# Attention loop of a convolution-and-attention kernel on one core: where sums, maxima and loads stand in the queues of each engine

## The reference, cut to what matters

```
q_in = quantile(x, 0.5) over the pixels;  x = x + relu(-q_in)
y = down2(relu(up2(x)))                       # 7-tap separable filter
spec = rfft2(y); gate = sigmoid(gelu(|spec| w1) w2); xf = y + irfft2(spec * gate)
q = xf @ q_w + q_b
k, v = two strided convolutions of xf (8x8 and 16x16), layer norm, kv_w, depthwise 3x3 on v
attn = softmax(q k / 4);  out = attn v @ proj_w + proj_b + y
```

## Time and profile before

| what | value |
|---|---|
| median of 3 runs | 11078.33 us (11071.28 to 11083.63) |
| the profiled execution's own time | 11074.85 us |
| span of its trace | 11073.5 us |
| instructions | 198462 |
| mean granted TensorE clock | 0.956 of 2.4 GHz |
| PE, DVE, ACT, POOL busy | 90%, 78%, 65%, 53% of the span |

### The profile page before, as it was taken

How to read it: one execution, slowest core, us unless ns; L and a number is a source line. 1 busy time by engine, 2 the same in 40 slices (tenths; PEclk the granted TensorE clock), 3 DMA queues, 4 the chain that set the end, 5 groups by cost and what they waited for, 6 DMA issues and landing times. The chain is left out here.

```text
span 11073.5 us, 198462 instructions
## 1 busy us (share of the span) xinstructions
PE 9980.4 (90%) x68713; PEld 4898.6 (44%) x68713; DVE 8648.7 (78%) x14529; ACT 7156.8 (65%) x12301; POOL 5870.6 (53%) x10577
## 2 busy tenths in 40 slices
PE   1998998989989899899989989899898998989989
PEld 1534535344353543535335353453534435354353
DVE  7877778877778777778777787777787777877777
ACT  5756666666666756667566675666667566675665
POOL 2374463745637365472754737446374553736547
PEclk9999999999999999999999999999999999999999
DMA  2031231312314032140322303123131331413214
GB/s 64 25 77 50 55 89 29 78 39 64 80 32 89 26 74 71 38 91 35 72 56 49 96 21 79 48 58 87 32 79 36 66 79 32 89 33 71 67 41 104
DMA packets 330611, 664.69 MB, mean 60 GB/s; under 512 B 95624, under 2 KB 241160, under 8 KB 308048
## 3 DMA queue, kind: packets, MB, share of 16 engines
q1 hardware_dynamic: 329552, 651.29, 24.7%
HBM read 232.53 MB, written 71.30 MB: 27 GB/s over the span
## 5 line engine op out<-in xcount | busy, mean ns | idle before, releaser
L1328 ACT ACTIVATE R<-ps 128x512 f32<-128x512 f32 x5120 | 2876.0, 593 | 1480.6 <-PE ps L816 1040.6
L1104 DVE TENSOR_REDUCE R<-ps 128x2 f32<-128x640 f32 x3840 | 3031.9, 818 | 757.6 <-PE ps L795 709.0
L269 ACT ACTIVATE R<-R,st 128x1475 bf16<-128x1475 f32 (+2 forms) x1326 | 2014.6, 1519 | 440.3 <-DVE st L343 415.0
L332 DVE TENSOR_SCALAR_CACHE_REDUCE R<-R,st 128x1255 bf16<-128x1255 f32 (+2 forms) x1326 | 2014.9, 1520 | 19.5 <-DVE st L343 0.2
L795 PE MATMUL ps<-KST,R 96*128 96x320 bf16 x7680 | 1703.0, 303 | 42.5 <-DMA R<-R 25.9
L841 PE MATMUL ps<-R 128*32 128x512 f32 x12288 | 1671.3, 617 | 0.0
L816 PE MATMUL ps<-R,KST 104*128 104x512 bf16 x4096 | 1599.3, 393 | 37.4 <-DMA R<-Wk 28.6
L1425 POOL TENSOR_TENSOR R<-R 128x256 f32<-128x256 f32 x1440 | 1054.6, 732 | 115.3
L1429 POOL TENSOR_TENSOR R<-R 128x256 f32<-128x256 f32 x1440 | 1046.9, 727 | 120.1
L795 PEld LDWEIGHTS ps<-KST,R 96*128 96x128 bf16 x7680 | 711.3, 99 | 759.0 <-DVE R L1104 283.0
L816 PEld LDWEIGHTS ps<-R,KST 104*128 104x128 bf16 x4096 | 396.9, 97 | 1083.6 <-ACT R L1328 748.6
(11 more groups left out here) (226 smaller groups left out, 19694.3 us busy)
## 6 DMA issues: line engine op xcount, KB each, us to landing
R<-R SPq DMA_DIRECT2D x3072, 64.0 KB, 2.4
R<-xh_in SPq DMA_DIRECT2D x136, 512.0 KB, 4.4
out_dram<-Z SPq DMA_DIRECT2D x68, 1024.0 KB, 3.9
R<-Wk SPq DMA_DIRECT2D x960, 64.0 KB, 2.0
Wk<-Wk SPq DMA_DIRECT2D x960, 64.0 KB, 2.0
R<-xa_in SPq DMA_DIRECT2D x36, 1024.0 KB, 10.0
R<-xb_in SPq DMA_DIRECT2D x36, 1024.0 KB, 11.7
R<-sr_in SPq DMA_DIRECT2D x32, 1024.0 KB, 5.0
```

The lines of the kernel that those rows point to most:

```text
L269: e.activation(junka[:, 2047:2048] if k == LONE else junka[:, 0:o2 - o1], xc[:, o1:o2], ACT.Sign, bias=mid, scale=-1.0, accum_out=ca[i]).t ...
L332: e.tensor_scalar(junk[:, 0:o1 - o0], xc[:, o0:o1], mid, None, ALU.is_le, ALU.add, accum_out=cv[i]).then_inc(md_cv, 1)
L1104: e.tensor_reduce(MX[(4 * u + s4) % 2][:, blk_, h0:h0 + 2], ps[:, 2 + 2 * bq:4 + 2 * bq, 0:320], axis=AX.X, op=ALU.max).then_inc(mx, 1)
L1328: e.activation(PB[:, t % 2, w, :], ps[:, w % 2, :], ACT.Exp).then_inc(ex, 1)
```

## The change

What it does, part by part:

1. On PE, `lay_max(t + 1)` moves from slot 0 to slot 3, on ACT from slot 1 to slot 3, and on DVE `split_max` moves from slot 8 of the tile before to slot 2 of the tile.
2. In SP's step, `lay_out(t - 1)` becomes the first thing, then come the loads of images, two DMAs of `load_unit`, then `lay_max(t + 1)`, then the remaining DMAs of `load_unit`.
3. The normalised sums get two buffers NO, the projection is of tile t - 4 and stands in slot 0, and `rest(t - 4)` in slot 2. The buffers ON and OX move to Wk.
4. The last three tiles, not two, are turned and divided by PE and DVE and need no `lay_out` or `normalise`; the first of them is divided at slot 3 of the last tile, ahead of the magnitudes (`largest`).
5. Unit 2 is loaded in steps 2 to 4 and unit 3 in steps 5 to 7, eight DMAs each; the first half of the image is loaded in two parts, at steps 28 and 29. The `stage` calls move by two slots.
6. Ahead of the loop, `slot` stands behind every second product of TAP1 and behind groups of six of TAP2, the first maxima are interleaved otherwise, and some `busy` products on the identity are added.

```
@@ constants
-STAGES = {(0, 2): (1, 0, 6), (0, 6): (1, 1, 6), (1, 2): (1, 2, 6), (1, 6): (1, 3, 6),
-          **{(8 * g - 12 + j, 2): (g, j, 6) for g in (2, 3) for j in range(4)}}
+STAGES = {(0, 4): (1, 0, 6), (0, 8): (1, 1, 6), (1, 4): (1, 2, 6), (1, 8): (1, 3, 6),
+          **{(8 * g - 12 + j, 4): (g, j, 6) for g in (2, 3) for j in range(4)}}
-LOADS = {u: 2 if u == 2 else 4 * u - 8 for u in range(2, 8)}
+LOADS = {**{3 * u - 4 + i: (u, 8 * i, 8 * i + 8) for u in (2, 3) for i in range(3)},
+         **{4 * u - 8 + i: (u, 6 * i, 6 * i + 6) for u in range(4, 8) for i in range(4)}}
+TURNED = 3
@@ tensor, keys
-                if n in (1, 3, 5):
-                    stage(0, n // 2 + 1, (4, 5, 3)[n // 2])
-                slot(1 if n > 5 else 0)
+                slot(n % 2)
+                if n in (3, 9, 15):
+                    stage(0, n // 6 + 1, (4, 5, 3)[n // 6])
@@ tensor, attention loop
-                    if w == (0 if t else 4) and t + AHEAD - 1 < NT:
+                    if w == 0 and t > 3:
+                        project_out(t - 4)
+                    if w == 3 and t + AHEAD - 1 < NT:
                         lay_max(t + AHEAD - 1)
                     if w in WEIGHS and t:
                         weigh(t - 1, WEIGHS.index(w))
-                    if w == 5 and t > 2:
-                        project_out(t - 3)
@@ vector, attention loop
-                    if w == 7 and t > 2:
-                        rest(t - 3, True)
+                    if w == 2 and t and t + AHEAD - 1 < NT:
+                        split_max(t + AHEAD - 1)
+                    if w == 2 and t > 3:
+                        rest(t - 4, True)
                     if w < 8 and ahead < NT:
                         maxima(ahead // 4, ahead % 4, w)
-                    if w == 8 and ahead < NT:
-                        split_max(ahead)
                     if w == 8 and t:
                         sums(t - 1)
@@ scalar, attention loop
-                    if w == (1 if t else 4) and t + AHEAD - 1 < NT:
+                    if w == 3 and t + AHEAD - 1 < NT:
                         lay_max(t + AHEAD - 1)
@@ gpsimd
                 if t:
-                    e.wait_ge(po_ps, t)
+                    e.wait_ge(on, t)
+                if t > 1:
+                    e.wait_ge(po_ps, t - 1)
...
-                e.tensor_tensor(XN2, XO[k], XI, ALU.mult).then_inc(on, 1)
+                e.tensor_tensor(NO[k], XO[k], XI, ALU.mult).then_inc(on, 1)
@@ sync, attention loop
-                if t + AHEAD - 1 < NT:
-                    lay_max(t + AHEAD - 1)
+                if 0 < t <= NT - TURNED:
+                    lay_out(e, t - 1)
+                if t >= NT - 4 and t < NT - 2:
+                    e.wait_ge(sc_ps, 280)
+                    load_next(e, it, 0, part=t - NT + 4)
...
-                if u == 7 and s4 == 0:
-                    e.wait_ge(sc_ps, 280)
-                    load_next(e, it, 0)
-                for v, t0 in LOADS.items():
-                    if t0 <= t < t0 + 4:
-                        load_unit(e, v, 6 * (t - t0), 6 * (t - t0) + 6)
-                if 0 < t < NT - 1:
-                    lay_out(e, t - 1)
+                v, n0, n1 = LOADS.get(t, (0, 0, 0))
+                if n1:
+                    load_unit(e, v, n0, n0 + 2)
+                if t + AHEAD - 1 < NT:
+                    lay_max(t + AHEAD - 1)
+                if n1:
+                    load_unit(e, v, n0 + 2, n1)
```

More of the change, by code:

```diff
@@ L156, in program @@
         XD = [R2[:, 1024 + 256 * i:1280 + 256 * i] for i in range(2)]
-        XI, XN2, ON, OX = (R2[:, 1536 + 256 * i:1792 + 256 * i] for i in range(4))
+        XI, XN2, *NO = (R2[:, 1536 + 256 * i:1792 + 256 * i] for i in range(4))
+        ON, OX = W[:, 1536:1792], W[:, 1792:2048]
         RD = [R2[:, 2640 + 16 * i:2656 + 16 * i] for i in range(2)]
@@ L877, in tensor @@
             lay_max(0)
-            for k in range(16, 20):
+            for k in range(14, 20):
                 first_maxima(k)
+                busy(0, 1)
+            busy(0, 4)
             for t in range(NT):
@@ L1081, in vector @@
                 stage(0, j, (6, 4, 5, 3)[j])
-                slot((4, 4, 4, 13)[j])
+                slot((3, 3, 4, 6)[j])
             first, second = keys(0), keys(1)
             next(first)
-            slot(1)
+            slot(3)
             next(first)
-            slot(1)
+            slot(3)
             next(first, None)
-            slot(1)
-            for k in range(8):
+            slot(6)
+            for k in range(4):
                 first_maxima(k)
             next(second)
-            first_maxima(8)
-            first_maxima(9)
+            first_maxima(4)
+            first_maxima(5)
             next(second)
-            first_maxima(10)
+            first_maxima(6)
+            first_maxima(7)
             next(second, None)
-            for k in range(11, 20):
+            for k in range(8, 20):
                 first_maxima(k)
@@ L1279, in keys @@
                              ACT.Identity, bias=c(f"v{n}b", 64)).then_inc(ka[s], 1)
+                yield
                 if s == 0:
@@ L1296, in scalar @@
             next(first)
-            bias(56, 64).then_inc(zb, 1)
+            bias(25, 37)
+            next(first)
+            bias(37, 52)
+            next(first)
+            bias(52, 62)
             next(first, None)
-            next(second)
-            next(second, None)
+            bias(62, 64).then_inc(zb, 1)
+            for _ in range(4):
+                next(second, None)
             def lay_max(t):
@@ L1307, in lay_max, with turned @@
                 e.activation(MR[t % 2], pb[0:8, :], ACT.Copy).then_inc(mr, 1)
+            def turned(t):
+                n = t - NT + TURNED
+                e.wait_ge(ot_ps, n + 1)
+                if n:
+                    e.wait_ge(po_ps, t)
+                e.activation(OX, ps[:, 4 + t % 2, 0:256], ACT.Copy).then_inc(ox, 1)
             def values():
@@ L1334, in scalar @@
                         stage(*STAGES[t, w])
-            for n in range(2):
-                e.wait_ge(ot_ps, n + 1)
-                if n:
-                    e.wait_ge(po_ps, NT - 2 + n)
-                e.activation(OX, ps[:, 4 + n, 0:256], ACT.Copy).then_inc(ox, 1)
+                    if t == NT - 1 and w == 7:
+                        turned(NT - 3)
+            turned(NT - 2)
+            turned(NT - 1)
         def gpsimd(e):
```

108 lines of the change are left out of this document (66 added, 42 removed).

## The result

The changed kernel takes 15283.25 us (median of 4 runs, 15278.3 to 15285.26) against 11078.11 us (11071.28 to 11083.63, 4 runs) for the kernel before: a ratio of 1.3797 [1.3779, 1.3814]. That is 4205 us more, 262.8 for each of the 16 images. The forecast was 15,150 us, by 255 an image.

What follows compares the result with a forecast made beforehand. The prediction took PE to bound the attention loop; per image, 194.5 us for the chain plus 72.5 for the clock less 12 of gains made +255, over 16 images +4080, forecast 15,150 us, range 14,300 to 15,900.

Steps and rivals of the forecast that it cites:

- The chain: Attention loop: `weigh`'s end, sums copy, `lay_out` issues, unit issues, `lay_max` landing, next scores run serially; +194.5 us an image.
- everything outside the 29 tiles: Gains from the change's other parts, ahead of the loop and in the tail: -12 us an image.
- The work in a tile: Attention loop, first scores to the end of `weigh`'s last third: 8.4 us, with 8.6 and 8.2 as ends.
- The links: Between `weigh`'s end and the next scores: copy 0.8, issue 0.03, four issues 2.43, unit loads 1.44, landing 2.52 us.
- The image DMAs: Loads ahead of `lay_max`: 0.7 us each for single ones; steps 28 and 29 add 1.3 and 3.8 each.
- The clock: Attention loop: idle gaps lower PE's clock for 5.2 us of each tile, costing 2.5 us a tile, +72.5 an image.
- the clock stays up: Rival, attention loop: the same chain without any clock loss, +2920 us, 14,000 us; chance 0.08.
- low throughout: Rival, attention loop: the same chain with the clock low through each tile, +5936 us, 17,010 us; chance 0.06.
- Taps untied: Ahead of the loop: PE does TAP2 products while waiting for median pieces, -5 us an image.
- the first tile: Start of the attention loop: `busy` products let the first tile run at the high clock, -2 us an image.
- Turned tiles and projection: Tile 30 and tail: three turned tiles and later projection remove PE's waits for POOL's normalising, -5 us an image.
- The rival "faster": Attention loop: SP does not reach `lay_out` late, the landing stays hidden, -16 us an image, 10,820 us; chance 0.05.

Runs made afterwards that it cites:

- experiment 1: The changed kernel with `lay_out(t - 1)` last in SP's step again, behind `lay_max(t + 1)`: 11065.79 us, 0.9987 of before.
- experiment 2: The kernel before with only `lay_out(t - 1)` moved to the front of SP's step: 14893.8 us.
- experiment 8: The changed kernel with 24 identity products on PE in each tile's wait and the image DMAs behind `lay_max`: 13909.34 us.
- experiment 3: The changed kernel with 24 identity products on PE behind the last scores of tiles 1 to 29: 14535.83 us.
- experiment 7: The kernel before with only the edits ahead of the attention loop (part 6 of the change): 10944.28 us, ratio 0.9884.
- experiment 6: The changed kernel with `lay_out` last in SP's step and POOL's `add_median` left out of the attention loop: 10924.77 us.
- experiment 9: The changed kernel with the old places of maxima and stages, SP's old order, projection in slot 5 and `rest` in slot 7: 10758.91 us, ratio 0.9711.
- experiment 10: The kernel before with only the maxima later, split in slot 2, turning and copy in slot 3: 11471.77 us, ratio 1.0356.

## Why the prediction was right, and where its sizes were off

**The chain.** Right, and shown: undoing the move takes 4217 us away (experiment 1), making it alone adds 3816 (experiment 2). The marks came as forecast: 464 waits for the DMA of `lay_max`, 6.6 us of idle time, 3.77 us from the first `lay_out` to `lay_max`, 17.4 us a tile, clock 0.847 for "about 0.8", PE 72% where 65% was said, since PE at the low clock is busy for longer (its 9980 us of before would be 65% of the new span).

**Its sum, an image.** Predicted 540.5 us for the 29 tiles (468 and 72.5), measured 553.8. That the two agree so nearly is in part luck, for the sum holds errors of both signs:

| term | predicted | measured | from |
|---|---|---|---|
| tiles at the high clock, without the delay by images | 452 | 465.9 | experiment 8 |
| image DMAs ahead of `lay_max` | 16 | 25.3 | the change and experiment 8 |
| the low clock | 72.5 | 62.6 | the change and experiment 8 |
| everything outside the 29 tiles | -12 | -17 | windows above |

- *The work in a tile* is the term that was off most. It was put at 8.4 us from the first scores to the end of `weigh`, with 8.6 and 8.2 as the ends; at the full clock it measured 8.88 (experiment 8), outside both. That is 0.48 us in each of 29 tiles, 13.9 in all. A tile that starts drained is thus no shorter than one in full flow, which had 8.61; my 8.4 supposed that it would be. It is 0.27 us longer, as much as a plain tile of experiment 1 is longer than one before. The links came to 6.96 in the tile shown, where 7.2 was said (2.40 for 2.52 of landing, 1.2 for 1.44 of unit loads). With the other figure for the landing that the prediction gives, 2.0 us, the sum would have been short by another half a microsecond a tile.
- *The image DMAs.* I priced the eight small ones by their issue alone, 0.7 us, and only the two at steps 28 and 29 by a late landing, of 3.8. In the trace of the change, from the issue of `lay_max` to the scores, the median is 2.48 us in the tiles without an image DMA, 4.21 behind those of steps 16 to 19, 3.54 behind those of 24 to 27, and 6.47 behind the pairs at 28 and 29. The last was priced about right (6.35); nothing in it was special to the end of the loop, and the same delay, smaller, behind the eight small loads was left out: some 11 us an image.
- *The range* of 14,300 to 15,900 is narrower than its own ends added up, -61 and +76 us an image, which give 14,170 and 16,370; the time lies in both.
- *The clock* costs 2.16 us a tile and not 2.5. Its stretch at the lower level was taken as 5.2 us in each tile. In the tile shown slots stand 0.96 us apart from 1709.35 to 1710.31, and by 1715.15 the scores take 0.38; over the 29 tiles the granted clock from first scores to the end of `weigh` is 0.80 on average, which is a low stretch of 4.6 us a tile. The rivals "the clock stays up" and "low throughout" are out: the one would have nothing to win back in experiments 3 and 8, the other 188.5 us an image, and the clock cost 62.6.

**The other parts.** Taps untied, and the first tile: -5 and -2 predicted, -8.0 and -2.5 measured; the edits ahead of the loop alone give 8.4 in both together (experiment 7). The waits that they were to remove were 5.9 us an image, as was read, and are gone; what gave the rest was not taken apart. Turned tiles and projection: -5 predicted, -6.6 in the tail. No wait for POOL's normalising is left there.

**What the prediction missed** stands in its sentence that unit loads, two buffers and later stages are "nothing here", hidden under the chain, and "were that cover gone they might give another 3 to 5". The first half held. For the second, with the cover gone the whole of the loop's edits cost 17.3 us an image (experiment 1), because of the later maxima, which I had left out of that sentence, and of the image loads ahead of `lay_max`. The maxima cost 0.27 us in most plain tiles, more in the stage tiles, and 6.6 where they fall on `add_median`; the loads cost some 2 in tile 28 (experiment 6). Only with maxima, projection, stages and SP's order as they were does the loop gain, 2.7 us (experiment 9). Why a plain tile loses 0.27 us with the split in slot 2 was not taken apart. That `rest` moved to slot 2 as well is not needed for it, since experiment 10 leaves `rest` in slot 7 and shows the same 0.27.

**The rival "faster"** had the right condition: SP would have to get the sums 6.4 us ahead of the next scores, and it gets them at the end of the tile. Its figure of 10,820 us for a kernel in which the chain is absent was not far from what experiment 9 reached, 10,759, but by luck: the rival kept the later maxima and the new slots, and with these experiment 1 measured 11,066.

## What to carry to other kernels

Before a step is moved to the front of a queue, find when its own wait ends and what stands behind it with a nearer due date: here a DMA whose data was ready at 1713.75, when ACT's copy ended, went out at 1722.56, behind four that waited for the end of the tile, and one queue's order was worth 3816 us. Price such a chain link by link from rows, put large loads behind the small DMA that an engine waits for, and expect the clock to take something more for each gap. When a stall covers everything else, the edits beside it look free: measure each again once the stall is gone, and move slots that share a PSUM bank only together.

## What the runs showed of the hardware

- **A small operation of DVE stood still beside POOL.** L1097, 16 elements a partition, took 1.82 us instead of 0.18, and ended within 0.03 us of POOL's operation of 1.90 us, which had started 0.11 us before it. It happened 71 times in experiment 1, and what hangs on it was worth 6.6 us in the 29 tiles of the image shown (289.9 against 283.3). Shorter operations of POOL do the same: in experiment 10, 306 of the 512 splits began while POOL's L1425 (0.73 us) ran, and every one ended 0.03 to 0.04 us behind its end, at 0.59 to 0.65 us instead of 0.18. Who starts first matters: in the kernel before, 342 splits saw an operation of POOL begin during them, and all kept 0.18 us. The kernel before pays for it too: its tiles 19, 21 and so on to 27 take 9.28 us, their neighbours 8.88, and in these tiles of every image the split takes some 0.67 us beside POOL's L1429; that the one causes the other was not tested. The Trainium skill, page "SBUF — State Buffer", section "SBUF: two separate sides", says that a VectorE operation with two SBUF inputs and a GpSimd operation that reads SBUF exclude each other from a shared pair of ports for the whole instruction. By that rule the small operation waits for the large one's end, and the rows beside L401, L1425 and L1429 agree; 11 splits of experiment 1 that began beside POOL's L1489 kept 0.18 us, and no run here took the ports themselves apart from other causes.
- **A small DMA lands later behind a large load that SP issued ahead of it.** In the changed kernel the scores start 2.41 to 2.55 us behind the issue of `lay_max` in the tiles without an image DMA, unit loads ahead or not, and 3.28 to 5.02 us behind it with a part of an image (512 KB) ahead, 6.17 to 6.85 with the two DMAs of steps 28 and 29. With these loads right behind it the same ten tiles have 2.43 to 2.60 (experiment 8).
- **A gap in every tile keeps the clock low for only a part of the next.** After some 6.6 us of idle time the slots ran at 1.2 GHz for the first 3.1 to 6.5 us of tiles 2 to 29, 4.6 on average over the loop, which cost 62.6 us an image. 24 products in the gap brought the granted clock to 0.98, for 98 us more of PE's work an image, and 53.3 us less of time; where they left 4.67 us of the gap empty the next tile began at the lower level again (experiment 3), and where they left 1.41 us it did not (experiment 8).
